# Channel attention of a two-layer decoder on one Trainium2 core: turned scores signalled head by head, and two VectorE instructions moved behind the negation

## The chip, the cores and the metric

The kernel runs on one core of one Trainium2 chip, as one launch. The metric is device time in microseconds (us) of that core, the median over several runs. The engines are TensorE (PE; its weight loads are listed as PEld), VectorE (DVE), ScalarE (ACT), GpSimd (POOL) and SyncE (SP), whose queue issues the DMAs. A "q" behind an engine's name is its sequencer.

## The reference, cut to what matters

The whole reference is a stack of six sublayers on `x` (32, 64, 256), each with a layer norm in front and added back to `x`. The edited part is the fifth, attention over channels:

```python
def _L1_xattn_ref(qkv, y):            # both (32, 64, 256)
    N_HEADS = 16
    bs, width, length = qkv.shape     # 32, 64, 256
    ch = width // N_HEADS             # 4
    q = qkv.reshape(bs * N_HEADS, ch, length)
    k = v = y.reshape(bs * N_HEADS, ch, -1)
    scale = 1.0 / math.sqrt(math.sqrt(ch))
    weight = jnp.einsum('bct,bcs->bts', q * scale, k * scale)
    weight = jax.nn.softmax(weight.astype(jnp.float32), axis=-1)
    a = jnp.einsum('bts,bcs->bct', weight, v)
    return a.reshape(bs, -1, length)

x = x + _L1_xattn_ref(_layernorm(x, axis=-1), ctx_2048)
```

There are 512 heads of 4 channels. Each head has a 256 x 256 matrix of scores, a softmax over it, and a product with the 4 channels of the context.

## The kernel before, in words

**Tiling.** The 2048 tokens are 16 tiles of 128 rows (TILES), 32 heads each. A tile is worked on in 8 slots (CH_SETS), a slot being 4 heads, one in each group of 32 partitions (CH_RGS). Half a tile is 4 slots (CH_HALF). There are 128 slots and 32 halves. Queries and keys are split into f16 parts and laid out by many small DMAs (qp and kp, a ring of 4 tiles).

**Two passes over the scores.** `scores` (L1496) makes the scores of two heads with queries on the partitions (L1502), and VectorE takes each row's maximum (`top`, L1589 to L1593: a reduction of 128 x 1024 values). After 4 slots the 32 columns of maxima are transposed by TensorE (L1547), negated by VectorE into `mT` (L1616), and brought by a DMA (`load_max`, L1431 to L1434) into row 31 of each group of the queries. `scores_turned` (L1506) then makes the same scores with keys on the partitions and the maximum subtracted, since row 31 takes part in the contraction (L1510). ScalarE takes the exponential of each head (L1578), and TensorE multiplies by the values, with a row of ones for the totals (L1558).

**The order of the work.** It is written out by hand in steps n, two to a slot. `tensor_step` (L1514) issues the scores of pair n%2 of slot t = n//2, the turned scores of slot b, 6.5 slots behind (CH_B_LAG = 13 steps), the transpose at the first step of every fourth slot, and a half of the value product of slot c, 8 slots behind (CH_C_LAG = 16). All instructions of an engine run in the order written. Scores use two pairs of PSUM banks in turn, and the transpose takes a turn in that order too (`bank`, `a_first`, `a_turn`, `a_second`). Turned scores use a ring of three banks T, a bank to a head. The waits that matter:

- TensorE, before any score matmul of a step: `s_maxed` (the pair of banks has been read), and `s_exped` for both heads of the pair of turned scores (L1531 to L1533). The four matmuls of scores and the four of turned scores are interleaved (L1534 to L1542), and one count of `s_scoredT` tells of both heads.
- ScalarE: `s_scoredT` for the pair (L1574), then a head's exponential. Once a half it copies the output out of PSUM (L1587).
- VectorE, `vector_step` (L1605): the maximum of the step; at every fourth slot the negation; in the second step of the sixth slot of a tile `invert` (L1595, the reciprocal of the totals of two tiles ago, which waits for their load); in the second step of the fourth slot `measured` (L1601, the layer-norm statistics of three tiles ago, L227 in a helper, which wait for `s_finished`).
- SP, `sync` (L1430), one iteration per tile n: the maxima of the odd half, a weight block of the next stage (`stage`, L186 in a helper), values (`load_v`, L1428, which waits for `s_vset` of GpSimd), the store of an odd half's output (`store_out`, L1438), keys (L1347), the totals of tile n-2 (`load_total`, L1445, which waits until the output has been stored), five query loads (L1423), the maxima of the even half (L1434), a weight block, an output store, four query loads, the store of the reciprocals (`store_inverse`, L1449, which waits for `invert`), three query loads, and the load of output and reciprocals of tile n-2 (`load_out`, L1455 and L1456).
- GpSimd, `gpsimd` (L1687), one iteration per tile: the normalised queries of tile+2, splitting of weight blocks, the values of the even half (`set_v`, L1678), `finish` of tile-2 (L1683 multiplies by the reciprocals, L1685 adds to `x` and counts `s_finished`), then the values of the odd half, for which SP's `load_v` waits.

"Even" and "odd" below mean the half: the even half of a tile is its first, and its negation falls at t % 8 == 4; the negation of the odd half falls at t % 8 == 0 of the next tile.

Of the kernel before, what the change touches and what calls it, by code (L numbers as in the profile page):

```python
# [15 lines left out]
P = 128  # L16
B, S, D = 32, 64, 256
TOKENS = B * S
KD = D // P
TILES = TOKENS // P  # L20
# [1351 lines left out]
def channel_stage(core, keys, moe, jobs=(), first=0):  # L1372
# [39 lines left out]
    def bank(user):  # L1412
        return A[user % 2]
# [3 lines left out]
    def load_q(sp, tile, parts):  # L1417
        sp.wait_ge(s_lo, tile + 1)
        if tile >= CH_RING:
            sp.wait_ge(s_scoredT, 2 * CH_SETS * (tile - CH_RING + 1))  # L1420
        for n in parts:
            p, ch = n // CH_CH, n % CH_CH
            sp.dma_start(qp[n:P:32, tile % CH_RING], xs[ch:P:CH_CH, tile % 2, p % 2]).then_inc(q_in[tile % 2], 16)  # L1423
# [6 lines left out]
    def sync(sp):  # L1430
# [33 lines left out]
        for n in range(TILES + 3):  # L1464
            if 0 <= 2 * n - 1 < CH_HALVES:
                load_max(2 * n - 1)
            stage(2 * n - 1)
            if 2 <= n + 1 < TILES:
                load_v(sp, n + 1)
            if n == 3:  # L1470
                moe.load_constants(sp)
            if 0 <= 2 * n - 3 < CH_HALVES:
                store_out(2 * n - 3)
            if CH_KEYS_AHEAD <= n + 2 < TILES:
                sp.wait_ge(s_scoredT, 2 * CH_SETS * max(0, n + 2 - CH_RING + 1))
                sp.wait_ge(k_in[n % 2], 16 * CH_RGS * (n // 2 + 1))
                keys.load(sp, n + 2, k_in[n % 2])
            if 0 <= n - 2 < TILES:
                load_total(n - 2)
            if n + 2 < TILES:  # L1480
                load_q(sp, n + 2, range(5))
            if 2 * n < CH_HALVES:
                load_max(2 * n)
            stage(2 * n)
            if 0 <= 2 * n - 2 < CH_HALVES:
                store_out(2 * n - 2)
            if n + 2 < TILES:
                load_q(sp, n + 2, range(5, 9))
            if 0 <= n - 2 < TILES:
                store_inverse(n - 2)  # L1490
            if n + 2 < TILES:
                load_q(sp, n + 2, range(9, CH_KEYROWS))
            if 0 <= n - 2 < TILES:
                load_out(n - 2)
# [8 lines left out]
                                    kp[rows, tile % CH_RING, set8, :], start=True, stop=True)  # L1503
        return last

    def scores_turned(t, pair, u):  # L1506
        tile, set8 = t // CH_SETS, t % CH_SETS
        for g in (2 * pair, 2 * pair + 1):
            rows = slice(32 * g, 32 * (g + 1))
            last = nc.tensor.matmul(ps[:, T[(t * CH_RGS + g) % len(T)], u * D:(u + 1) * D], kp[rows, tile % CH_RING, set8, u * P:(u + 1) * P],  # L1510
                                    qp[rows, tile % CH_RING, set8, :], start=True, stop=True)
        return last

    def tensor_step(pe, n):  # L1514
        t, pair = n // 2, n % 2
        tile = t // CH_SETS
        b, b_pair = (n - CH_B_LAG) // 2, (n - CH_B_LAG) % 2
        if t < CH_SLOTS:
            if n % (2 * CH_SETS) == 0:
                pe.wait_ge(q_in[tile % 2], 16 * CH_KEYROWS * (tile // 2 + 1))  # L1520
                pe.wait_ge(k_in[tile % 2], 16 * CH_RGS * (tile // 2 + 1))
            user = (a_first, a_second)[pair](t)
            if user >= 2:
                pe.wait_ge(s_maxed, user - 1)
        if 0 <= b < CH_SLOTS:
            if b == 0 and b_pair == 0:
                pe.wait_ge(*keys.accumulated)
            if b % CH_HALF == 0 and b_pair == 0:
                half = b // CH_HALF
                pe.wait_ge(m_in[half % 2], 16 * (half // 2 + 1))  # L1530
            done = b * CH_RGS + 2 * b_pair + 2 - len(T)  # L1531
            if done > 0:
                pe.wait_ge(s_exped, done)  # L1533
        for u in range(KD):  # L1534
            if t < CH_SLOTS:
                last = scores(t, pair, u)
                if u == KD - 1:
                    last.then_inc(s_scored, 1)
            if 0 <= b < CH_SLOTS:
                last = scores_turned(b, b_pair, u)  # L1540
                if u == KD - 1:
                    last.then_inc(s_scoredT, 1)  # L1542
        if pair == 0 and t % CH_HALF == 0 and 0 < t <= CH_SLOTS:
            half = t // CH_HALF - 1
            user = a_turn(half)
            pe.wait_ge(s_maxed, max(user - 1, a_second(t - 1) + 1))
            nc.tensor.transpose(ps[0:32, bank(user), 0:P], m[:, half % 2].rearrange("p g s u -> p (g s u)"), core.ident).then_inc(s_scored, 1)  # L1547
        c, u = (n - CH_C_LAG) // 2, (n - CH_C_LAG) % 2
        if 0 <= c < CH_SLOTS:
            half, j = c // CH_HALF, c % CH_HALF  # L1550
# [19 lines left out]
    def scalar(act):  # L1570
        for b in range(CH_SLOTS + CH_HALF):
            for g in range(CH_RGS):
                if b < CH_SLOTS:
                    act.wait_ge(s_scoredT, 2 * b + g // 2 + 1)  # L1574
                    if g == 0 and b >= 3:
                        act.wait_ge(s_mixed, b - 2)
                    n = b * CH_RGS + g
# [27 lines left out]
    def vector_step(dve, n):  # L1605
# [4 lines left out]
        if pair == 0 and t % CH_HALF == 0 and t > 0:  # L1610
# [3 lines left out]
            if half >= 2:  # L1614
                dve.wait_ge(m_in[half % 2], 16 * (half // 2))
            nc.vector.tensor_scalar(mT[:, half % 2], ps[0:32, bank(user), 0:P], -1.0, None, ALU.mult).then_inc(s_maxed, 1)  # L1616
        if pair == 1 and t % CH_SETS == 5 and tile >= 2:
            invert(dve, tile - 2)
        if pair == 1 and t % CH_SETS == 3 and tile >= 3:
            measured(dve, tile - 3)  # L1620

    def settle_tiles(dve, tiles):
        done, count = settle(core, dve, f"ch{tiles[0]}", 3, tiles)
# [937 lines left out]
```

## Time and profile before

| what | value |
|---|---|
| median of 3 runs | 1916.67 us (1914.07 to 1920.19) |
| the profiled execution | 1911.81 us |
| its span, first to last instruction | 1910.0 us |
| PE busy | 1707.1 us (89%), 15840 instructions |
| DVE busy | 1489.9 us (78%), 2884 instructions |
| ACT busy | 1031.2 us (54%), 2056 instructions |
| POOL busy | 720.3 us (38%), 965 instructions |
| the edited stage | about 1143 to 1502 us of the span |

The shares are means over six sublayers with different limits, so they don't tell what limits the edited stage. A line is that of the kernel; L227 and L186 are lines of helpers. Times in the rows count from the start of the span.

### The profile page before, as it was taken

The page shows a single profiled execution, that of the slowest core. Times are in us where ns is not written, and L with a number is a line of the kernel's source. Part 1 is how long each engine was busy: PE and PEld are TensorE (multiplying, and loading weights), DVE is VectorE, ACT ScalarE, POOL GpSimd, SP SyncE. Part 2 cuts the span into 40 slices and gives each one's busy share as a digit, 9 for nine tenths or more (in the row PEclk, how much of TensorE's full clock was granted, in tenths as well). Part 3 has the DMA queues.
Part 4 walks back from the last instruction along what each step waited for, and adds up shares of the span by engine and source line. Part 5 has one row for each costly group of instructions (what it writes and reads, how often), then busy time and mean ns, then how long its engine had stood idle before and what let it go on. Part 6 is the DMA issues. An engine that isn't in the chain of part 4 may idle for free.

```text
span 1910.0 us, 43448 instructions
## 1 busy us (share of the span) xinstructions
PE 1707.1 (89%) x15840; PEld 1004.0 (53%) x15840; DVE 1489.9 (78%) x2884; ACT 1031.2 (54%) x2056; POOL 720.3 (38%) x965
## 2 busy tenths in 40 slices
PE   5999999689999999979977996777777889999998
PEld 2656665347777777755544551222222356656555
DVE  6866666579989899857886889999999478676654
ACT  3665655345555555534436765888888533323222
POOL 4635321387677677612345453444531000000000
PEclk9999999889999999989989997999999999999999
DMA  9601110000000000000001211333321023222121
GB/s 254 177 24 51 29 41 2 17 23 12 10 13 14 7 10 4 2 9 1 1 1 36 59 38 52 94 91 96 96 72 41 17 76 96 88 63 72 63 83 50
DMA packets 87662, 94.92 MB, mean 50 GB/s; under 512 B 17568, under 2 KB 63264, under 8 KB 87456
## 3 DMA queue, kind: packets, MB, share of 16 engines
q1 hardware_dynamic: 83712, 87.76, 16.3%
q8 instruction: 128, 2.10, 0.5%
q10 hardware_dynamic: 2976, 2.32, 0.5%
q0 software_dynamic: 768, 2.10, 0.4%
q14 instruction: 78, 0.64, 0.1%
HBM read 78.51 MB, written 10.22 MB: 46 GB/s over the span
## 4 chain that ended last, share of the span: by engine, by line
DVE 23%; PE 22%; issue 6%; POOL 3%; ACT 1%; DVEq 0%; POOLq 0%; ACTq 0%
PE ps L275 18%; DVE arena L1592 14%; POOL arena L1147 2%; PE ps L1859 1%; PE ps L1502 1%; PE ps L1856 1%; DVE arena L2440 1%; DVE arena L2436 0%; DVE arena L1201 0%; DVE arena L244 0%; POOL arena L2013 0%; DVE arena L2371 0%; DVE arena L2369 0%; DVE arena L1952 0%; ACT arena L2312 0%
## 5 line engine op out<-in xcount | busy, mean ns | idle before, releaser
L275 PE MATMUL ps<-arena 128*128 128x512 f16 (+6 forms) x6464 | 1090.9, 324 | 54.6 <-POOL arena L1147 9.6
L275 PEld LDWEIGHTS ps<-arena 128*128 128x128 f16 (+1 forms) x6464 | 602.1, 99 | 442.0 <-issue 37.8
L1578 ACT ACTIVATE arena<-ps 128x512 f32<-128x512 f32 x512 | 278.6, 598 | 71.1 <-PE ps L1510 48.5
L1592 DVE TENSOR_REDUCE arena<-ps 128x4 f32<-128x1024 f32 x256 | 305.3, 1218 | 10.8 <-PE ps L1502 10.5
L1502 PE MATMUL ps<-arena 31*128 31x256 f16 x1024 | 102.2, 275 | 72.7 <-ACT arena L1578 52.1
L1558 PE MATMUL ps<-arena 128*32 128x256 f32 x2048 | 164.1, 392 | 2.7 <-ACT arena L1587 0.6
L2430 DVE TENSOR_TENSOR arena<-ps,arena 128x512 f32<-128x512 f32 x96 | 66.1, 688 | 126.8 <-ACT arena L2322 111.6
L2322 ACT ACTIVATE arena<-ps 128x512 f32<-128x512 f32 x96 | 57.1, 596 | 176.9 <-PE ps L275 176.4
L1502 PEld LDWEIGHTS ps<-arena 31*128 31x128 f16 x1024 | 34.8, 92 | 187.6 <-DVE arena L1592 151.0
L1051 POOL TENSOR_TENSOR arena<-arena 128x512 f32<-128x512 f32 x96 | 98.8, 1043 | 45.1 <-DVE arena L221 44.0
L652 POOL TENSOR_TENSOR arena<-arena 128x256 f32<-128x256 f32 x64 | 39.5, 617 | 180.4 <-DVE arena L617 180.4
L508 ACT ACTIVATE arena<-ps,arena 128x512 f32<-128x512 f32 x64 | 44.0, 687 | 113.6 <-PE ps L275 113.6
L1510 PE MATMUL ps<-arena 32*128 32x256 f16 x1024 | 101.0, 275 | 0.9 <-ACT arena L1578 0.2
L2312 ACT ACTIVATE arena<-arena 128x512 f16<-128x512 f32 x96 | 60.1, 626 | 73.7 <-DVE arena L2436 73.3
L1147 POOL TENSOR_TENSOR arena<-arena 128x512 f16<-128x512 f32 x32 | 50.2, 1575 | 113.3 <-ACT arena L1304 109.9
L197 POOL TENSOR_TENSOR arena<-arena 128x256 f16<-128x256 f32 (+5 forms) x72 | 86.1, 1196 | 5.8
L1065 POOL TENSOR_TENSOR arena<-arena 128x256 f32<-128x256 f32 x80 | 58.2, 728 | 74.4 <-DVE arena L982 74.1
L916 ACT ACTIVATE arena<-ps 128x512 f16<-128x512 f32 x64 | 38.2, 597 | 81.5 <-PE ps L842 81.5
L195 POOL CAST arena<-arena 128x256 f16<-128x256 f32 (+5 forms) x72 | 45.3, 629 | 96.6 <-DMA arena<-in_L_ffn_gate_up_proj 67.3
L981 DVE TENSOR_TENSOR arena<-ps,arena 128x512 f32<-128x512 f32 x80 | 54.9, 686 | 31.7 <-ACT arena L911 24.4
L1056 POOL TENSOR_TENSOR arena<-arena 128x512 f32<-128x512 f32 x64 | 67.5, 1055 | 27.9 <-DVE arena L1017 27.8
L565 DVE TENSOR_TENSOR arena<-ps,arena 128x512 f16<-128x512 f32 x64 | 43.8, 684 | 39.1 <-ACT arena L497 39.1
(203 smaller groups left out, 2931.1 us busy)
## 6 DMA issues: line engine op xcount, KB each, us to landing
arena<-moe_cw SPq DMA_DIRECT2D x64, 192.0 KB, 2.8
arena<-moe_cw SPq DMA_DIRECT2D x64, 128.0 KB, 2.9
arena<-in_L_ffn_gate_up_proj SPq DMA_DIRECT2D x16, 384.0 KB, 3.4
ch_out<-arena SPq DMA_DIRECT2D x32, 128.0 KB
arena<-moe_cw SPq DMA_DIRECT2D x64, 64.0 KB, 2.7
ch_keys<-arena SPq DMA_DIRECT2D x48, 64.0 KB, 2.0
arena<-ch_keys SPq DMA_DIRECT2D x64, 48.0 KB
arena<-arena SPq DMA_DIRECT2D x192, 16.0 KB
```

The lines of the kernel that those rows point to most:

```text
L197: nc.gpsimd.tensor_tensor(lo, raw, hi, ALU.subtract).then_inc(core.s_split, 1)
L275: last = nc.tensor.matmul(out, a, b, start=start and n == 0, stop=stop and n == len(pairs) - 1, skip_group_check=not group)
L1051: nc.gpsimd.tensor_tensor(a4, a4, spread(rms[:, s % 2, u * CROSS_KVH:(u + 1) * CROSS_KVH], CROSS_HD), ALU.mult).then_inc(scaled.sem, 1)
L1056: nc.gpsimd.tensor_tensor(prob[:, k % 2], e[:, k % 2], spread(inv[:, k % 2, :], CROSS_KEYS), ALU.mult).then_inc(probs.sem, 1)
L1147: nc.gpsimd.tensor_tensor(hT[1][:, k % FFN_MEMBERS], h[:, k // FFN_MEMBERS % 2, k % FFN_MEMBERS], hT[0][:, k % FFN_MEMBERS], ALU.subtract) ...
L1502: last = nc.tensor.matmul(ps[:, bank(user) + n, u * D:(u + 1) * D], qp[rows, tile % CH_RING, set8, u * P:(u + 1) * P], kp[rows, tile % CH_ ...
L1510: last = nc.tensor.matmul(ps[:, T[(t * CH_RGS + g) % len(T)], u * D:(u + 1) * D], kp[rows, tile % CH_RING, set8, u * P:(u + 1) * P], qp[ro ...
L1558: last = nc.tensor.matmul(ps[32 * g:32 * (g + 1), O, 0:D], vz[:, half % 2, u, g, j, :], pT[:, c % 3, g, u, :], start=j == 0 and u == 0, st ...
L1578: nc.scalar.activation(pT[:, b % 3, g], ps[:, T[n % len(T)], :].rearrange("p (u t) -> p u t", u=KD), ACT.Exp, scale=CH_SCALE).then_inc(s_e ...
L1592: nc.vector.tensor_reduce(m[:, half % 2, 2 * half_pair:2 * half_pair + 2, j, :], ps[:, bank(user):bank(user) + 2, :].rearrange("p g (u s) ...
L2312: nc.scalar.activation(hT[0][:, b % 4, :], h[b % MOE_HELD], ACT.Copy).then_inc(s_hi, 1)
L2430: nc.vector.tensor_tensor(h[n % MOE_HELD], ps[:, U[n % 2], :], silu[:, n % 2, :], ALU.mult).then_inc(s_gated, 1)
```

## The change

Three things, all in the channel stage:

- TensorE: the turned scores of the pair's first head stay interleaved with the scores, behind a wait for that head's bank alone; those of the second head are issued after the transpose, behind a wait of their own, and ahead of the value product, which is last in the step. Each head counts `s_scoredT`, and every wait on it (ScalarE's, and those of SP before query and key loads) is rescaled from 2 to 4 counts a slot.
- VectorE: `invert` moves from the second step of slot 5 of a tile to directly behind the negation at slot 4.
- VectorE: `measured` moves from the second step of slot 3 to directly behind the negation at slot 0 of the tile, for the same tile-3.

```diff
     def load_q(sp, tile, parts):
...
-            sp.wait_ge(s_scoredT, 2 * CH_SETS * (tile - CH_RING + 1))
+            sp.wait_ge(s_scoredT, CH_RGS * CH_SETS * (tile - CH_RING + 1))
...
             if CH_KEYS_AHEAD <= n + 2 < TILES:
-                sp.wait_ge(s_scoredT, 2 * CH_SETS * max(0, n + 2 - CH_RING + 1))
+                sp.wait_ge(s_scoredT, CH_RGS * CH_SETS * max(0, n + 2 - CH_RING + 1))
...
-    def scores_turned(t, pair, u):
+    def scores_turned(t, g, u):
         tile, set8 = t // CH_SETS, t % CH_SETS
-        for g in (2 * pair, 2 * pair + 1):
-            rows = slice(32 * g, 32 * (g + 1))
-            last = nc.tensor.matmul(ps[:, T[(t * CH_RGS + g) % len(T)], u * D:(u + 1) * D], kp[rows, tile % CH_RING, set8, u * P:(u + 1) * P],
-                                    qp[rows, tile % CH_RING, set8, :], start=True, stop=True)
-        return last
+        rows = slice(32 * g, 32 * (g + 1))
+        return nc.tensor.matmul(ps[:, T[(t * CH_RGS + g) % len(T)], u * D:(u + 1) * D], kp[rows, tile % CH_RING, set8, u * P:(u + 1) * P],
+                                qp[rows, tile % CH_RING, set8, :], start=True, stop=True)
...
         b, b_pair = (n - CH_B_LAG) // 2, (n - CH_B_LAG) % 2
+
+        def bank_free(g):
+            done = b * CH_RGS + g + 1 - len(T)
+            if done > 0:
+                pe.wait_ge(s_exped, done)
+
...
-            done = b * CH_RGS + 2 * b_pair + 2 - len(T)
-            if done > 0:
-                pe.wait_ge(s_exped, done)
+            bank_free(2 * b_pair)
         for u in range(KD):
             if t < CH_SLOTS:
                 last = scores(t, pair, u)
                 if u == KD - 1:
                     last.then_inc(s_scored, 1)
             if 0 <= b < CH_SLOTS:
-                last = scores_turned(b, b_pair, u)
+                last = scores_turned(b, 2 * b_pair, u)
                 if u == KD - 1:
                     last.then_inc(s_scoredT, 1)
...
             nc.tensor.transpose(ps[0:32, bank(user), 0:P], m[:, half % 2].rearrange("p g s u -> p (g s u)"), core.ident).then_inc(s_scored, 1)
+        if 0 <= b < CH_SLOTS:
+            bank_free(2 * b_pair + 1)
+            for u in range(KD):
+                last = scores_turned(b, 2 * b_pair + 1, u)
+            last.then_inc(s_scoredT, 1)
         c, u = (n - CH_C_LAG) // 2, (n - CH_C_LAG) % 2
...
-                    act.wait_ge(s_scoredT, 2 * b + g // 2 + 1)
+                    act.wait_ge(s_scoredT, CH_RGS * b + g + 1)
...
             nc.vector.tensor_scalar(mT[:, half % 2], ps[0:32, bank(user), 0:P], -1.0, None, ALU.mult).then_inc(s_maxed, 1)
-        if pair == 1 and t % CH_SETS == 5 and tile >= 2:
-            invert(dve, tile - 2)
-        if pair == 1 and t % CH_SETS == 3 and tile >= 3:
-            measured(dve, tile - 3)
+            if t % CH_SETS == CH_HALF and tile >= 2:
+                invert(dve, tile - 2)
+            if t % CH_SETS == 0 and 3 <= tile < TILES:
+                measured(dve, tile - 3)
```

## Rows read from the trace of the kernel before

**Rows 1.** Chain of waits, 1130 to 1560 us, shares by line.

```profile
by line: DVE arena L1592 63.3%; issue 10.7%; PE ps L275 10.1%; PE ps L1502 3.2%; DVE arena L1599 1.7%; PE ps L1558 1.1%; POOL arena L2013 1.0%; ACT arena L1578 0.8%; DVE arena L244 0.6%; ACT L2322 0.6%; DVE arena L227 0.5%; PE ps L2207 0.5%
```

**Rows 2.** Table of lines, 1143 to 1502 us: busy us, mean ns, idle before.

```profile
L1592 DVE TENSOR_REDUCE arena<-ps 128x4 f32<-128x1024 f32 x256 | 305.3, 1218 | 10.8 <-PE ps L1502 10.5 <-DVE arena L221 0.2
```

**Rows 3.** Timeline, DVE, 1149 to 1156 us: start, us, instruction, idle before.

```profile
1149.62 5.73 DVE L1592 TENSOR_REDUCE arena<-ps 128x4 f32<-128x1024 f32 x5
```

**Rows 4.** Timeline, DVE, one tile from 1314 us, and the last maximum.

```profile
1314.09 0.27 DVE L1616 TENSOR_SCALAR arena<-ps 32x128 f16<-32x128 f32 x1
1314.66 8.51 DVE L1592 TENSOR_REDUCE arena<-ps 128x4 f32<-128x1024 f32 x7 [0.30 <-PE ps L1502]
1323.08 0.42 DVE L227 BATCH_NORM_STATS2 arena<-arena 128x6 f32<-128x256 f32 x1
1323.41 1.21 DVE L1592 TENSOR_REDUCE arena<-ps 128x4 f32<-128x1024 f32 x1
1324.54 0.27 DVE L1616 TENSOR_SCALAR arena<-ps 32x128 f16<-32x128 f32 x1
...
1328.68 0.54 DVE L1599 RECIPROCAL arena<-arena 128x64 f32<-128x64 f32 x1
...
1334.75 0.27 DVE L1616 TENSOR_SCALAR arena<-ps 32x128 f16<-32x128 f32 x1
...
1478.01 1.22 DVE L1592 TENSOR_REDUCE arena<-ps 128x4 f32<-128x1024 f32 x1
```

**Rows 5.** Timeline, one step from 1357 us, first ACT, then PE.

```profile
1357.24 1.09 ACT L1578 ACTIVATE arena<-ps 128x512 f32<-128x512 f32 x2
...
1358.46 0.60 ACT L1578 ACTIVATE arena<-ps 128x512 f32<-128x512 f32 x1
...
1357.99 0.28 PE L1502 MATMUL ps<-arena 31*128 31x256 f16 x2 [0.25 <-ACT arena L1578]
...
1358.10 0.28 PE L1502 MATMUL ps<-arena 31*128 31x256 f16 x2
1358.12 0.27 PE L1510 MATMUL ps<-arena 32*128 32x256 f16 x2
1358.32 0.42 PE L1558 MATMUL ps<-arena 128*32 128x256 f32 x4
```

**Rows 6.** Timeline, SP's queue, 1313 to 1336 us, DMAs issued.

```profile
1314.01 0.57 SPq L1456 DMA_DIRECT2D arena<-ch_inverse  x1
...
1319.23 0.39 SPq L1428 DMA_DIRECT2D arena<-in_ctxT  x1
...
1323.69 0.62 SPq L1445 DMA_DIRECT2D arena<-ch_out  x1
...
1327.36 0.56 SPq L1434 DMA_DIRECT2D arena<-arena  x1
...
1331.38 0.45 SPq L1449 DMA_DIRECT2D ch_inverse<-arena  x1
...
1334.48 0.57 SPq L1456 DMA_DIRECT2D arena<-ch_inverse  x1
```

**Rows 7.** Timeline, POOL, the final add of four tiles.

```profile
1235.56 0.72 POOL L1685 TENSOR_TENSOR arena<-arena 128x256 f32<-128x256 f32 x1
...
1317.88 0.73 POOL L1685 TENSOR_TENSOR arena<-arena 128x256 f32<-128x256 f32 x1
...
1401.20 0.72 POOL L1685 TENSOR_TENSOR arena<-arena 128x256 f32<-128x256 f32 x1
...
1442.47 0.73 POOL L1685 TENSOR_TENSOR arena<-arena 128x256 f32<-128x256 f32 x1
```

**Rows 8.** Timeline, PE, 1479 to 1480 us, steps without scores.

```profile
1479.59 0.64 PE L1558 MATMUL ps<-arena 128*32 128x256 f32 x8
1480.16 0.39 PE L1510 MATMUL ps<-arena 32*128 32x256 f16 x4
```

**Rows 9.** DMA issues, whole span: KB each, us from issue to landing.

```profile
ch_inverse<-arena SPq DMA_DIRECT2D x16, 32.0 KB, 2.5
```

## The prediction, made before the changed kernel ran

> **What bounds the kernel now.** I read the time and the span first: the profiled execution took 1911.81 us (span 1910.0), 4.86 us below the median of the runs, 1916.67. The sum is made against 1911.81 and then carried to the median. Only the stage of channel attention is edited, about 1143 to 1502 us. The chain of that stretch lies to 63.3% on VectorE's maximum over scores, L1592 [rows 1], and the table of lines has 256 of these at 1218 ns each [rows 2]. So VectorE seems to be the bound. The timeline corrects this. While no turned scores are in flight, five maxima take 5.73 us from the first start to the last end [rows 3]; with 1.22 for the last one that is (5.73 - 1.22) / 4 = 1.13 us apart. In the steady part seven take 8.51 us [rows 4]: 1.215 apart. The 0.085 us comes from a ring between ScalarE and TensorE [rows 5]. An exponential starts at 1357.24 and takes 0.60. It frees the bank for which the whole step on TensorE waits, scores included, and the score matmuls start at 1357.99. The last turned matmul starts at 1358.12 and takes 0.27, one signal then tells of both heads, and the next exponential starts at 1358.46. That is 1.22 us a step.
>
> A second loop hides behind this one. SP's queue and GpSimd fetch each tile's output back, and [rows 6, 7] have to be read together. SP issues the load of the inverse (L1456) at 1314.01. GpSimd's final add (L1685) runs from 1317.88 for 0.73, to 1318.61. Only then does SP get past its wait for the values (L1428, 1319.23). There follow the stores and key loads, the load of the totals (L1445, 1323.69), query loads, the load of the even half's maxima (L1434, 1327.36), the store of the inverse (L1449, 1331.38), and L1456 again at 1334.48. That turn took 20.47 us; over eight turns L1685 goes from 1235.56 to 1401.20, 20.71 each. VectorE's tile, from one odd negation to the next, is 1334.75 - 1314.09 = 20.66 [rows 4]. The two loops are equally long, and the second hardly waits for the first: the even negation ends at 1324.54 + 0.27 = 1324.81, 2.55 us before SP takes it up.
>
> **Part 1, heads signalled one at a time.** The ring is now over three banks, one head each, and the scores no longer stand behind the second bank. Two exponentials take 1.09 us with 0.60 for the second [rows 5], so ScalarE can start one every 0.49, 0.98 a step: not the bound. TensorE's step cost, in the old order, 0.33 from the first score matmul to the first of the value product (1357.99 to 1358.32, [rows 5]) and 0.57 from there to a next step that nothing holds (1479.59 to 1480.16, [rows 8]): 0.90. The second head now adds one or two rounds of 0.11 (1357.99 to 1358.10): 1.01 to 1.12. The added wait could cost a bubble of about 0.09, the 0.20 between 1358.12 and 1358.32 less one round; then it is up to 1.21. I take 1.12, since the rows show no bubble between matmuls of one kind; VectorE then sets 1.13. Behind the added wait stands the value product; it needs exponentials of older slots, so it isn't later than its inputs. The count of signals doubles, for which I see no cost.
>
> In each half turn two more matmuls come between the transpose and the value product. A change from 32-row to 32-column matmuls costs that same 0.09; two more of them in 31 half turns are 5.6 us if nothing hides them. VectorE has the reciprocal or the statistics to do at that place, so I take nothing and keep 5.6 as the far end. The Trainium skill (TensorEngine Tiling (Array Packing), Key Properties) says that switching the tiling mode drains the array, which speaks against this order; the trace agrees, with 0.09 us for one switch, and the sum by that rule would be the far end.
>
> **Part 2, the reciprocal behind the even negation.** After each negation VectorE stands 0.30 us for the second pair's scores [rows 4]. The reciprocal takes 0.54 (1328.68), of which 0.08 lies under its neighbour, as for the statistics, 0.42 long and 0.33 to the next start (1323.08 to 1323.41). So 0.30 of its 0.46 is hidden. But it needs the totals: issued at 1323.69 [rows 6], landed some 2.5 us later, the median to landing of the inverse's store, the nearest transfer of 32 KB [rows 9]. That is 1326.2, and the negation ends at 1324.81: at the old phase it would wait 1.4 us, 20 us over 14 tiles. I take nothing, since part 3 puts VectorE later against SP: totals land 1323.69 + 2.5 - 1318.61 = 7.6 us after L1685 ends, and the negation comes 9.7 us after it. The store of the inverse (1331.38) already stands 2.2 us and more behind the reciprocal in SP's order, so SP gains nothing from an earlier one.
>
> **Part 3, the statistics behind the odd negation.** This decides. They wait for L1685 of three tiles before. Until now they ran at 1323.08, 4.5 us after L1685's end at 1318.61. Behind the negation of 1314.09 they are wanted at 1314.36, 4.25 us before that end. Behind them on VectorE stand the second pair's maximum and all that follows, and so TensorE and ScalarE. VectorE waits, and the two loops become one. From F, the end of L1685:
> - to the statistics 0.05 (a hop; [rows 5] have 0.07 from matmul to exponential, the other end is nothing), the statistics 0.33, eight maxima 7 x 1.13 + 1.14 = 9.05, the even negation 0.27, the hop to SP 0.05: 9.75 to L1434;
> - SP alone reached it 1327.36 - 1318.61 = 8.75 after F;
> - from there to the next F as before: 20.71 - 8.75 = 11.96.
>
> The new turn is 21.71 us, 1.00 longer. VectorE's own tile would be 16 x 1.13 + 0.46 + 0.33 + 2 x 0.19 (0.27 less 0.08) = 19.25. What parts 1 and 2 win goes into the wait.
>
> **The sum.** Ahead of the first wait there is a gain: a half was 1334.75 - 1324.54 = 10.21 and becomes 9.05 + 0.57 (1314.09 to 1314.66) = 9.62. Two to three such halves reach SP before the first L1685: -1.5. Eight turns: +8.0. Two more, to the L1685 of 1442.47 [rows 7], where the weight loads are over: +1.8 (two of 1.00 less a little). That F comes at 1443.20 + 8.3 = 1451.5. The next finish isn't met: it is due 18 to 20 us on, VectorE 19.25. So the last statistics start at 1451.5 + 0.05 + 19.25 = 1470.8, the next maximum at 1471.1, and the last one 14 x 1.13 + 0.46 + 0.19 = 16.5 later, 1487.6. It was at 1478.01 [rows 4]: +9.6. The next stage opens on VectorE's work behind it, so this passes on. The trailing steps may give back 0.5 (nothing to 2). Total +9.1: 1920.9 for the profiled execution, 1925.8 against the median.
>
> **The rivals.**
> (a) The loops stay apart, since L1685 comes in time or SP's part shrinks. Then 19.25 replaces 20.71 in eleven turns, -16.1, and with -1.5 the time is 1899; with half of it 1908. Against it speak the 4.25 us. Chance 0.12.
> (b) One loop, but SP's stretch comes out about 1 us shorter, as its wait for the stored output (before 1323.69) may end sooner at the new phase. Then the turns stay 20.7 and the time is 1916. Chance 0.17.
> (c) Worse than the forecast: a step on TensorE is above 1.13, say 1.21, or the ring lives on. The eight maxima between F and SP's load then cost 0.6 more, 6.6 in eleven turns, and the first and last halves lose a gain of 3: 1935. Chance 0.13.
> (d) The forecast, turns of 21.4 to 22.0: 1920 to 1931. Chance 0.58.
>
> **How the numbers follow.** 0.3%, 5.75 us, is about what a measurement of this kernel can tell from no change. Of (d), 0.48 lies above that and 0.10 within; of (b), 0.13 is within and 0.02 on either side; (c) is slower, (a) faster. Slower 0.63, same 0.23, faster 0.14. The range, 1912 to 1935, takes in (d), most of (b) and half of (c), and leaves (a) out.
>
> **What would show it.** Right: about 2.4 us of idle time before most of the 13 statistics, released by L1685; L1685 every 21.7 us; SP waiting about 1 us for the negation at the even L1434; maxima 1.13 apart. Wrong: no such wait (then (a)), L1685 every 20.7 us (then (b)), maxima 1.2 apart behind the statistics (then (c)), or the reciprocal waiting for its totals.

## The result and the profile after

The changed kernel takes 1927.05 us (median of 6 runs, 1924.86 to 1931.13) where the kernel before takes 1915.57 us in the runs beside it. The ratio is 1.0068, with a 95% interval of 1.0053 to 1.0083: 0.7% slower. The forecast was 1925.8 and slower. It counted from a median of 1916.67 for the kernel before, so it forecast 9.1 us more; measured are 11.5 us more. The profiled execution took 1925.08 us. These are the span, the busy times and the chain of its page, and then the chain of the page of the kernel before:

```profile
span 1923.3 us, 43386 instructions
...
PE 1734.5 (90%) x15779; PEld 1013.2 (53%) x15840; DVE 1476.9 (77%) x2884; ACT 1026.7 (53%) x2056; POOL 719.6 (37%) x965
...
PE 24%; DVE 15%; issue 6%; POOL 3%; DMA 3%; SPq 3%; ACT 2%; DVEq 0%; POOLq 0%; ACTq 0%
```

```profile
DVE 23%; PE 22%; issue 6%; POOL 3%; ACT 1%; DVEq 0%; POOLq 0%; ACTq 0%
```

The chain now has 3% for DMA and 3% for SP's queue. Neither was in the chain before, nor in that of the stage [rows 1]. VectorE is busy for less time than before though the whole takes longer. The waits between 1165 and 1480 us say where it stands still (engine and line, what it waited for, us in total, times, the longest). SP's own waits follow in the second block:

```profile
DVE arena L227 <- POOL arena L1692: 28.5, 12, 4.3
...
PE ps L1502 <- ACT arena L1585: 0.7, 1, 0.7
```

```profile
SPq L1434 <- DVE arena L1623: 59.7, 26, 9.1
...
SPq L1444 <- DMA ch_out<-arena: 20.8, 12, 2.9
```

The first row of the first block is the one the prediction turned on: VectorE's statistics (L227) wait for GpSimd's final add (L1692, L1685 before), 12 times, 28.5 us, 2.4 each. Before, there was no such row. The second row is what the first part of the change has left of its wait. This is its counterpart in the kernel before:

```profile
PE ps L1502 <- ACT arena L1578: 51.2, 206, 0.8
```

And a little more than one tile of VectorE's timeline, to set beside [rows 4]:

```profile
1344.18 0.27 DVE L1623 TENSOR_SCALAR arena<-ps 32x128 f16<-32x128 f32 x1
1346.62 0.43 DVE L227 BATCH_NORM_STATS2 arena<-arena 128x6 f32<-128x256 f32 x1 [2.17 <-POOL arena L1692]
1346.96 4.64 DVE L1599 TENSOR_REDUCE arena<-ps 128x4 f32<-128x1024 f32 x4
1351.94 4.62 DVE L1599 TENSOR_REDUCE arena<-ps 128x4 f32<-128x1024 f32 x4 [0.34 <-PE ps L1502]
1356.48 0.27 DVE L1623 TENSOR_SCALAR arena<-ps 32x128 f16<-32x128 f32 x1
1356.68 0.53 DVE L1606 RECIPROCAL arena<-arena 128x64 f32<-128x64 f32 x1
1357.14 9.06 DVE L1599 TENSOR_REDUCE arena<-ps 128x4 f32<-128x1024 f32 x8
1366.13 0.27 DVE L1623 TENSOR_SCALAR arena<-ps 32x128 f16<-32x128 f32 x1
1368.46 0.43 DVE L227 BATCH_NORM_STATS2 arena<-arena 128x6 f32<-128x256 f32 x1 [2.07 <-POOL arena L1692]
```

The negation ends at 1344.45, and the statistics start at 1346.62, 2.17 us later. Behind them four maxima take 4.64 us. The eight of the next half take 9.06, which is (9.06 - 1.20) / 7 = 1.12 us apart, no longer 1.215. The reciprocal (L1606) starts 0.20 us after the start of the even negation and waits for nothing. GpSimd's final adds in this stretch:

```profile
1345.75 0.73 POOL L1692 TENSOR_TENSOR arena<-arena 128x256 f32<-128x256 f32 x1
...
1367.59 0.73 POOL L1692 TENSOR_TENSOR arena<-arena 128x256 f32<-128x256 f32 x1
```

The add ends at 1346.48, and the statistics start 0.14 us after. From one such end to the next it is 21.84 us here. From SP's queue, as in [rows 6]:

```profile
1356.78 0.56 SPq L1434 DMA_DIRECT2D arena<-arena  x1
```

The load of the even maxima (L1434) starts at 1356.78, just after the negation of 1356.48, and 10.30 us after the end of the add; before, it stood in SP's own order at 8.75. From there the queue's order is that of before, and the next add ends at 1368.32, 11.54 us on. So the two loops have become one.

### The profile page after: what moved, and what is told of

Read it like the earlier page. It is cut to its first block, busy times and chain, and to the rows that moved or that the text cites. A ratio compares the mean times of both kernels' runs of the same rounds, so it can differ in the third digit from the quotient of the medians.

```text
span 1923.3 us, 43386 instructions
## 1 busy us (share of the span) xinstructions
PE 1734.5 (90%) x15779; PEld 1013.2 (53%) x15840; DVE 1476.9 (77%) x2884; ACT 1026.7 (53%) x2056; POOL 719.6 (37%) x965
## 4 chain that ended last, share of the span: by engine, by line
PE 24%; DVE 15%; issue 6%; POOL 3%; DMA 3%; SPq 3%; ACT 2%; DVEq 0%; POOLq 0%; ACTq 0%
PE ps L275 18%; DVE arena L1599 6%; DMA arena<-ch_inverse 2%; SPq L1423 2%; POOL arena L1147 2%; PE ps L1565 1%; DMA ch_inverse<-arena 1%; PE ps L1866 1%; PE ps L1502 1%; PE ps L1863 1%; DVE arena L2447 1%; DVE arena L2443 0%; POOL arena L1692 0%; DVE arena L1201 0%; POOL arena L1690 0%
## 5 line engine op out<-in xcount | busy, mean ns | idle before, releaser
L1585 ACT ACTIVATE arena<-ps 128x512 f32<-128x512 f32 x512 | 273.5, 598 | 87.2 <-PE ps L1509 85.1
L1599 DVE TENSOR_REDUCE arena<-ps 128x4 f32<-128x1024 f32 x256 | 292.9, 1206 | 4.6 <-PE ps L1502 4.1
L1565 PE MATMUL ps<-arena 128*32 128x256 f32 x2048 | 174.3, 415 | 0.5 <-ACT arena L1594 0.4
L2329 ACT ACTIVATE arena<-ps 128x512 f32<-128x512 f32 x96 | 57.1, 596 | 177.1 <-PE ps L275 176.6
L1502 PE MATMUL ps<-arena 31*128 31x256 f16 x1024 | 107.0, 292 | 46.3 <-DVE arena L1599 44.1
L1509 PE MATMUL ps<-arena 32*128 32x256 f16 x1024 | 132.7, 287 | 0.0
L1502 PEld LDWEIGHTS ps<-arena 31*128 31x128 f16 x1024 | 29.6, 94 | 166.4 <-DVE arena L1599 130.0
```

The lines of the kernel that those rows point to most:

```text
L1502: last = nc.tensor.matmul(ps[:, bank(user) + n, u * D:(u + 1) * D], qp[rows, tile % CH_RING, set8, u * P:(u + 1) * P], kp[rows, tile % CH_ ...
L1509: return nc.tensor.matmul(ps[:, T[(t * CH_RGS + g) % len(T)], u * D:(u + 1) * D], kp[rows, tile % CH_RING, set8, u * P:(u + 1) * P], qp[ro ...
L1565: last = nc.tensor.matmul(ps[32 * g:32 * (g + 1), O, 0:D], vz[:, half % 2, u, g, j, :], pT[:, c % 3, g, u, :], start=j == 0 and u == 0, st ...
L1585: nc.scalar.activation(pT[:, b % 3, g], ps[:, T[n % len(T)], :].rearrange("p (u t) -> p u t", u=KD), ACT.Exp, scale=CH_SCALE).then_inc(s_e ...
L1599: nc.vector.tensor_reduce(m[:, half % 2, 2 * half_pair:2 * half_pair + 2, j, :], ps[:, bank(user):bank(user) + 2, :].rearrange("p g (u s) ...
```

## The experiments

Each kernel was timed in interleaved runs with the kernel before. Beside the time I use one length of the trace: the fourteen tiles from the first tile's odd negation to the fifteenth's, 1169.38 to 1459.62 in the kernel before, 20.73 us a tile. What lies around the stage is left out of it. It is an average over unlike tiles, read from one profiled execution of each kernel, so a tenth or two of it mean little.

| kernel | median us | ratio, interval | us a tile |
|---|---|---|---|
| before | 1913 to 1917 | 1 | 20.73 |
| the change | 1927.05 | 1.0068 (1.0053 to 1.0083) | 21.64 |
| statistics back | 1914.82 | 1.0005 (0.9990 to 1.0021) | 20.87 |
| statistics only | 1932.03 | 1.0086 (1.0058 to 1.0114) | 22.03 |
| heads only | 1916.82 | 1.0014 (0.9995 to 1.0033) | 20.85 |
| reciprocal only | 1913.70 | 0.9997 (0.9980 to 1.0014) | 20.82 |
| statistics of four tiles ago | 1918.88 | 1.0006 (0.9990 to 1.0023) | 20.77 |
| SP's order only, on before | 1914.29 | 0.9996 (0.9981 to 1.0011) | 20.68 |
| SP's order, on the change | 1922.59 | 1.0045 (1.0030 to 1.0061) | 21.73 |
| four tiles ago and SP's order | 1910.80 | 0.9969 (0.9952 to 0.9985) | 20.25 |
| the same, constants late | 1906.49 | 0.9958 (0.9942 to 0.9975) | 19.99 |
| the same, reciprocal back | 1903.30 | 0.9956 (0.9939 to 0.9973) | 19.89 |
| constants late, heads in pairs | 1914.11 | 1.0005 (0.9992 to 1.0018) | 20.69 |

**The statistics back at their old place**, on the changed kernel:

```diff
-            if t % CH_SETS == 0 and 3 <= tile < TILES:
-                measured(dve, tile - 3)
...
+        if pair == 1 and t % CH_SETS == 3 and tile >= 3:
+            measured(dve, tile - 3)
```

> The changed kernel with the statistics put back into the second step of the tile's fourth slot; heads signalled singly and the reciprocal behind the even negation stay. Theory (the statistics' wait merged the two loops): the statistics have no idle time before them, GpSimd's final add comes every 20.7 us again, since SP's own loop is left as the bound, maxima stand 1.13 us apart inside a half, and the 11 turns of 21.8 us fall back to 20.7. VectorE is ahead of SP, so either the reciprocal waits for the totals or TensorE for the even half's maxima. Time 1903 to 1912 us. Rival (the new order on TensorE costs the time: switches between 32-row and 32-column matmuls, a fuller step, lower clock): still slower than before, 1920 to 1927 us.

The slowdown is gone, so the statistics' place is its cause and TensorE's new order isn't. But the time is that of before; the gain that I expected, to 1903 to 1912 us, didn't come. GpSimd's final adds are 20.75 us apart, as before. VectorE, faster now, is held at another place. These are its wait at the reciprocal and, from SP's waits, that for the stored output:

```profile
DVE arena L1606 <- DMA arena<-ch_out: 13.1, 9, 4.2
```

```profile
SPq L1444 <- DMA ch_out<-arena: 21.1, 12, 2.8
```

VectorE waits nine times for the totals that SP loads (13.1 us). SP in turn stands 21.1 us for the landing of the output, a part of its own loop. SP's loop is what is left as the bound; that is a reading of these waits here, and the versions with SP's order changed test it below.

**The statistics alone**, on the kernel before:

```diff
+            if t % CH_SETS == 0 and 3 <= tile < TILES:
+                measured(dve, tile - 3)
...
-        if pair == 1 and t % CH_SETS == 3 and tile >= 3:
-            measured(dve, tile - 3)
```

> The kernel before with the statistics alone moved behind the odd negation. Theory: VectorE waits at 12 or 13 statistics, about 1.5 to 2 us each; from the end of GpSimd's final add to SP's load of the even maxima it is 0.05 + 0.33 + 7 x 1.215 + 1.14 + 0.27 + 0.05 = 10.35 us, since the ring of pairs still holds maxima 1.215 apart, so a turn is 10.35 + 11.96 = 22.3 us, 1.6 longer than 20.7; in eleven turns +17.6 us, less what the hidden 0.30 us give: 1928 to 1936 us, slower than the change with all three parts. Rival (the statistics are harmless, TensorE's order is what costs): 1911 to 1918 us.

It is slower than before by 0.86%, as the theory has it, and slower than the full change a tile (22.03 to 21.64). The rival falls. One assumption was wrong: the maxima behind the wait. This is one wait and the eight maxima behind it in that kernel's timeline:

```profile
1395.81 0.43 DVE L227 BATCH_NORM_STATS2 arena<-arena 128x6 f32<-128x256 f32 x1 [1.69 <-POOL arena L1685]
1396.15 9.12 DVE L1592 TENSOR_REDUCE arena<-ps 128x4 f32<-128x1024 f32 x8
1405.19 0.27 DVE L1616 TENSOR_SCALAR arena<-ps 32x128 f16<-32x128 f32 x1
```

Eight take 9.12 us, 1.13 apart, though the ring of pairs is still there: TensorE's steps in this half start at 1401.06, 1402.27 and 1403.48, 1.21 apart. While VectorE waited, TensorE had got ahead by the scores of a step, and eight maxima don't use up that lead. It is so behind nine of the thirteen statistics; behind the other four, where the granted clock falls to 0.50, the eight take 0.5 to 1.1 us more. So a turn was 22.07, not 22.3.

**Heads alone**, on the kernel before (VectorE's program stays as it was; the cut leaves out the counts of `s_scoredT`, rescaled as in the change):

```diff
-            done = b * CH_RGS + 2 * b_pair + 2 - len(T)
-            if done > 0:
-                pe.wait_ge(s_exped, done)
+            bank_free(2 * b_pair)
...
-                last = scores_turned(b, b_pair, u)
+                last = scores_turned(b, 2 * b_pair, u)
...
+        if 0 <= b < CH_SLOTS:
+            bank_free(2 * b_pair + 1)
+            for u in range(KD):
+                last = scores_turned(b, 2 * b_pair + 1, u)
+            last.then_inc(s_scoredT, 1)
```

> The kernel before with the heads' part alone (issue, wait and signal one head at a time); reciprocal and statistics at their old places. Theory: maxima go from 1.215 to 1.13 us apart, TensorE no longer waits for an exponential ahead of scores; VectorE's tile would be 16 x 1.13 + 0.46 + 0.33 + 2 x 0.57 = 20.0 us, but SP's loop keeps 20.6 to 20.7, so only the tiles before and behind the loop's stretch and what the phase allows are won: 1903 to 1912 us. Rival (drains and a fuller TensorE step): 1917 us or more, maxima 1.2 apart or idle time of VectorE before them.

**Reciprocal alone**, on the kernel before:

```diff
-        if pair == 1 and t % CH_SETS == 5 and tile >= 2:
-            invert(dve, tile - 2)
+            if t % CH_SETS == CH_HALF and tile >= 2:
+                invert(dve, tile - 2)
```

> The kernel before with the reciprocal alone moved behind the even negation. Theory: VectorE reaches it ahead of the totals (issued 1323.69, landed about 1326.2, negation done at 1324.81), so it waits in most tiles, first about 1.4 us and then what keeps VectorE in step with SP's loop of 20.7 us; nothing or up to 2 us is won: 1913 to 1918 us. Rival (no wait, 0.30 us hidden in each of 14 tiles): 4.2 us less than before, 1911 to 1912 us. Rival on the other side (the 1.4 us are paid in each of 14 tiles): 1930 us or more.

With single heads the maxima stand 1.13 apart, and yet a tile takes 20.85 us. Final adds are 20.84 apart. Single heads alone win nothing, and they cost nothing that these runs can tell. The gain that I expected around SP's stretch, 1903 to 1912 us, didn't come, and the median, 1916.82, is within 0.2 us of where my rival began, which also named idle time of VectorE. There is such idle time, but not for the rival's reason. Below are VectorE's waits for scores in this kernel (10.0 us in 31 waits in the kernel before), then the longest of them, with SP's load of the even maxima and TensorE's next matmul, and last an ordinary wait behind a negation:

```profile
DVE arena L1599 <- PE ps L1502: 20.0, 43, 2.1
```

```profile
1226.59 0.56 SPq L1434 DMA_DIRECT2D arena<-arena  x1
...
1228.43 0.28 PE L1502 MATMUL ps<-arena 31*128 31x256 f16 x2 [3.42 <-issue]
...
1228.86 1.23 DVE L1599 TENSOR_REDUCE arena<-ps 128x4 f32<-128x1024 f32 x1 [2.12 <-PE ps L1502]
...
1339.14 8.01 DVE L1599 TENSOR_REDUCE arena<-ps 128x4 f32<-128x1024 f32 x7 [0.30 <-PE ps L1502]
```

The wait behind a negation, where the two added matmuls and the switches are, is 0.30 us as in [rows 4]. The added idle time is in a few long waits. In the longest TensorE stands 3.42 us. The trace names no releaser, but in the kernel this step waits for the landing of the even maxima, which SP issued at 1226.59. So it is SP's queue that VectorE meets. Five of the fourteen tiles are free of such waits and take 19.99 us, where my expectation had 20.0.

The reciprocal alone changes nothing either, as expected, but its wait is small, 4.1 us in five waits, not 1.4 in each tile:

```profile
DVE arena L1599 <- DMA arena<-ch_out: 4.1, 5, 1.3
```

**The statistics of four tiles ago**, on the changed kernel, so that they stay behind the odd negation and don't wait:

```diff
-            if t % CH_SETS == 0 and 3 <= tile < TILES:
-                measured(dve, tile - 3)
+            if t % CH_SETS == 0 and 4 <= tile < TILES:
+                measured(dve, tile - 4)
...
         else:
+            if k == 2:
+                measured(dve, TILES - 4)
             measured(dve, TILES - 5 + k)
```

> The changed kernel, but the statistics behind the odd negation are those of four tiles ago, not three; the thirteenth tile's join the ones left for the next stage. Theory: their release came a whole turn earlier (about 16 us before), so they never wait; SP's own loop, 20.7 us a turn, is the bound that is left, as with the statistics at their old place: 1910 to 1917 us, no more than 0.3% off the kernel before. Rival (SP's loop isn't a bound, the putting back of the statistics merely lost their 0.30 us of cover): VectorE's tile of 19.25 us comes out, 1895 to 1903 us.

The median, 1918.88, lies 2 us above my range, but against the runs beside it (1914.43) the ratio is 1.0006: no difference from the kernel before, as the theory has it, and far from the rival's 1903. It isn't the place on VectorE that costs, but the release that it waits for. The wait at the statistics is gone, and what VectorE waits for now is the totals that SP loads:

```profile
DVE arena L1606 <- DMA arena<-ch_out: 17.0, 11, 4.3
```

**SP's order.** Now the other loop. SP stood for the landing of the output before it loaded the totals; three of the five query loads go ahead of it:

```diff
+            if n + 2 < TILES:
+                load_q(sp, n + 2, range(3))
             if 0 <= n - 2 < TILES:
                 load_total(n - 2)
             if n + 2 < TILES:
-                load_q(sp, n + 2, range(5))
+                load_q(sp, n + 2, range(3, 5))
```

On the kernel before:

> The kernel before with one edit in SP's queue: three of the five query loads are issued ahead of the load of the totals, so that SP doesn't stand about 1.6 us for the landing of the output. Theory of two equal loops: SP's turn falls from 20.7 to about 19.2 us, but VectorE's tile stays at 20.66, so nothing or up to 2 us is won: 1911 to 1917 us, and SP now waits for the negation at the even load of maxima in most tiles. Rival (SP's loop alone is the bound): 11 turns of 1.5 us, 1897 to 1901 us.

SP's waits in the kernel before, and in this one:

```profile
SPq L1434 <- DVE arena L1616: 32.8, 9, 9.0
SPq L1444 <- DMA ch_out<-arena: 19.0, 11, 2.9
```

```profile
SPq L1434 <- DVE arena L1618: 65.2, 27, 9.2
...
SPq L1444 <- DMA ch_out<-arena: 5.6, 2, 2.9
```

The landing costs 5.6 us and no longer 19.0, SP waits 27 times for the negation and no longer 9, and the time is the same. Shortening SP's loop alone is worth nothing, as shortening VectorE's alone was.

On the changed kernel:

> The changed kernel with the three query loads ahead of the load of the totals and nothing else. Theory of the merged loop: the edit shortens a stretch of SP's queue that already ends in a wait for the even negation, about 1.1 us of it per turn; that wait gets longer, and the turn of 21.8 us stays: 1923 to 1929 us. Rival (SP's length is what the statistics wait for): 11 turns shorter by 1.5 us, 1908 to 1913 us.

Its wait at the statistics, and SP's own waits:

```profile
DVE arena L227 <- POOL arena L1694: 27.0, 12, 3.0
```

```profile
SPq L1434 <- DVE arena L1625: 77.3, 28, 9.3
...
SPq L1444 <- DMA ch_out<-arena: 2.8, 1, 2.8
```

SP gets rid of its wait for the landing here too (2.8 us, 20.8 in the changed kernel) and waits more for the negation instead (77.3, 59.7 in the changed kernel). VectorE still waits 27.0 us for the final adds, and a tile takes 21.73. The median, 1922.59, lies 0.4 us below my range, and the interval of the ratio, 1.0045, overlaps that of the change. The merged loop goes through VectorE at this place; the part of SP's queue that the edit shortens isn't in it.

On the version with the statistics of four tiles ago:

> Both: the changed kernel with the statistics of four tiles ago and the three query loads ahead of the load of the totals. Theory of two loops: now both are shorter, VectorE 19.25 us a tile, SP about 19.2, with a wait of a few tenths of VectorE's reciprocal for the totals: turns of 19.4 to 19.8 us, about a microsecond less in each of 12, and 1 to 3 us at the ends: 1898 to 1906 us, faster than every other version. Rival (something third holds the tile at 20.6, such as TensorE's step or DMA traffic): 1911 us or more.

VectorE's wait at the reciprocal (L1608 here):

```profile
DVE arena L1608 <- DMA arena<-ch_out: 10.3, 7, 4.3
```

This is faster than the kernel before, by 0.3%, so both loops together were the bound. My range was missed by 5 us. The tile is 20.25, not 19.6, although six of the fourteen take 19.28, VectorE's own length: from the odd negation at 1235.94 to that at 1255.22, for one. VectorE waits 10.3 us at the reciprocal, of that 4.3 at one place, where SP's queue also loads the constants of the next stage. And what follows the last maximum takes 437.65 us against 432.01. The stretch from 1470 to 1490 us, here and in the kernel before (length; busy us and instructions of PE, PEld, DVE, ACT, POOL; granted clock; DMA share, GB/s), has a clock of 0.74 for 1.00:

```profile
1470.00:1490.00 20.00, 17.15 (x147) 5.70 (x147) 8.78 (x34) 12.61 (x26) 2.05 (x6) 0.74 0.08 23
```

```profile
1470.00:1490.00 20.00, 15.33 (x208) 5.26 (x209) 15.17 (x41) 16.24 (x31) 2.07 (x6) 1.00 0.11 32
```

The two stretches don't hold quite the same work, since the stage ends 6 us earlier here. Two other versions tell what such a fall is worth: with the constants late and with the statistics back the same stretch has 0.74 and 0.75, and there what follows the last maximum takes 434.20 and 433.30 us. So the clock makes about 2 of the 5.6 us at most, and what makes the rest in this one execution stays open.

**Constants late.** The three versions built on it:

```diff
-            if n == 3:
+            if n == 12:
                 moe.load_constants(sp)
...
-            if tile == 4:
+            if tile == 13:
                 moe.set_up(pool)
```

> The version with the statistics of four tiles ago and three query loads ahead of the load of the totals, and in addition the constants of the next stage are loaded in SP's thirteenth iteration and set up in GpSimd's fourteenth, no longer in the fourth and fifth. There the reciprocal of the fourth tile waited 4.3 us for its totals and that turn took 23.0 us. Theory: that wait falls to under 1 us and the last maximum comes 4 to 5 us earlier, since VectorE takes that in time: 1904 to 1908 us. Rival (SP catches up anyway, or the late constants hold the next stage back): no change, 1909 to 1913 us.

The reciprocal's waits fall from 10.3 to 6.5 us. The longest was to fall below 1 us and is 3.3, at the constants' new place, so it has moved more than it has gone:

```profile
DVE arena L1608 <- DMA arena<-ch_out: 6.5, 7, 3.3
```

It comes out at 1906.49; against the version without this edit (1910.80) the intervals overlap, so that this edit is worth 4 us is likely and not shown.

The same with the reciprocal at its old place:

```diff
-            if t % CH_SETS == CH_HALF and tile >= 2:
-                invert(dve, tile - 2)
...
+        if pair == 1 and t % CH_SETS == 5 and tile >= 2:
+            invert(dve, tile - 2)
```

> The same with late constants, but the reciprocal at its old place, in the second step of slot 5. Theory: it never waits for its totals, and costs 0.46 uncovered, of which 0.30 was hidden behind the negation; where it waited up to 2 us per tile in its new place the time is won back. VectorE's tile is 19.6 us and even: within 2 us of the version with the reciprocal behind the negation, 1904 to 1910 us. Rival (the reciprocal's waits lie on the path that bounds the tiles): 3 us or more faster than that version.

The ratio is 0.9956, with 0.9958 for the version before. The median, 1903.30, is 3.2 us lower and 0.7 us below my range, but the intervals nearly coincide: a difference between the reciprocal's two places isn't shown, and one of 3 us isn't ruled out. These two are the fastest versions of the study, 0.4% ahead of the kernel before.

And the constants-late version with the turned scores in pairs, as in the kernel before:

```diff
-            bank_free(2 * b_pair)
+            done = b * CH_RGS + 2 * b_pair + 2 - len(T)
+            if done > 0:
+                pe.wait_ge(s_exped, done)
...
-        if 0 <= b < CH_SLOTS:
-            bank_free(2 * b_pair + 1)
-            for u in range(KD):
-                last = scores_turned(b, 2 * b_pair + 1, u)
-            last.then_inc(s_scoredT, 1)
```

> The same with late constants, reciprocal behind the negation, statistics of four tiles ago and SP's reorder, but TensorE's heads in pairs as in the kernel before. Theory: with SP's loop out of the way the ring of pairs is the bound, maxima 1.215 apart; VectorE's tile is 16 x 1.215 + 0.46 + 0.33 + 0.4 less what catches up, 20.2 to 20.6 us, so 0.8 us a tile slower than with single heads: 1910 to 1915 us. Rival (single heads never paid, SP's reorder alone makes the gain): the same time as with single heads.

With pairs the ring of [rows 5] is back. These are the score matmuls (L1504 here) waiting for an exponential:

```profile
PE ps L1504 <- ACT arena L1580: 51.1, 203, 0.8
```

There are 203 such waits, 51.1 us, and a tile of 20.69 against 19.99. The intervals of the two ratios, 1.0005 and 0.9958, are apart. So single heads are worth 0.7 us a tile, 0.5% of the time, as soon as SP's loop is out of the way, and nothing measurable while it isn't.

## Why the prediction was right

**The loops.** That the two loops were equally long and that the second hardly waits for the first was right. The kernels that shorten only one of them (heads alone, reciprocal alone, SP's order alone, statistics of four tiles ago) and the putting back of the statistics have ratios within 0.15% of 1, with intervals that reach 0.33%. That the second loop is SP's is shown by its order: with VectorE's loop already short, changing it takes the tile from 20.77 to 20.25 us.

**Part 1.** Maxima at 1.13 came as predicted. A step on TensorE at full clock in the changed kernel, and the start of a later one and of the one behind it:

```profile
1352.41 0.28 PE L1502 MATMUL ps<-arena 31*128 31x256 f16 x2
1352.42 0.28 PE L1509 MATMUL ps<-arena 32*128 32x256 f16 x1
...
1352.54 0.48 PE L1509 MATMUL ps<-arena 32*128 32x256 f16 x3
1352.95 0.42 PE L1565 MATMUL ps<-arena 128*32 128x256 f32 x4
...
1356.62 0.28 PE L1502 MATMUL ps<-arena 31*128 31x256 f16 x2
...
1357.53 0.28 PE L1502 MATMUL ps<-arena 31*128 31x256 f16 x2
```

Here the second head adds two rounds: 0.54 from the first score matmul to the value product (1352.41 to 1352.95), where it was 0.33. With the 0.57 behind it the step is 1.11; I took 1.12. That is the long case. The step from 1356.62 to 1357.53 is 0.91, and the second head adds nothing to it. So TensorE had more room than I gave it.

The switches at the transpose stayed covered. The time can't show it, since the interval of the heads alone reaches 1.0033, which is 6.3 us. VectorE's waits can: behind a negation they are 0.30 us with the heads alone, as before, and in the changed kernel all its waits for scores in the stretch are 3.6 us, where they were 10.0. So the far end of 5.6 us wasn't reached. The Trainium skill (TensorEngine Tiling (Array Packing), Key Properties) says that a change of tiling mode drains the array. The rows agree as far as the 0.09 us of the prediction go; here none of it reached VectorE.

**Part 2.** Right in the changed kernel, where the reciprocal never waited. The 20 us that I named for the old phase were far off: alone it waited 4.1 us in all. The longest wait, 1.3 us, is about the 1.4 that I had, but I let it be paid 14 times. VectorE, once held back, is later in the next tile too; that this is why most tiles don't wait is argued and not tested.

**Part 3.** 12 of 13 statistics waited (predicted: most), 2.4 us each (predicted 2.4). The turn, over eight from the second final add to the tenth, is 21.84 us (predicted 21.71, 20.70 before). Its parts: to SP's even load 10.06 on average (predicted 9.75), from there on 11.78 (predicted 11.96). Two errors of opposite sign cancel in part, so that the turn is nearer than its parts.

**The sum.** The last maximum came 12.6 us later (1478.01 to 1490.58), where I had 9.6. The differences are terms of the sum. The early gain of 1.5 us didn't come: the first final add ends at 1213.02 in both. The turn with the constants took 23.91 for 23.26, +0.6. The eight turns cost 9.1 instead of 8.0, the two behind them 1.4 instead of 1.8. The trailing 0.5 wasn't given back; what follows the last maximum took 432.7 for 432.0. In all it is +13.3 between the two profiled executions and +11.5 in the medians, against +9.1. That the forecast of 1925.8 lies only 1.3 us from 1927.05 is in part luck: the median it was counted from, 1916.67, came out 1.1 us lower in more runs.

**The rivals.** (a), that the loops stay apart, is what happens when the statistics don't wait; but its price was wrong. I let VectorE's own 19.25 us a tile come out, 1899 us. The runs without the wait stay at 20.8, since SP's own loop is there whatever VectorE does. The prediction had that loop in its first part and forgot it where the final add merely comes in time; only with a shorter SP part as well do tiles of 19.28 appear, and then in six of fourteen. (c) was wrong in its mechanism as far as the ring goes: in the kernel with the statistics alone, which still has the ring, the maxima behind a wait stand 1.13 apart.

## What to carry to other kernels

An instruction moved into an idle gap brings its wait along: ask when its releaser comes, not only whether the gap is wide enough, because on an engine that runs in order everything behind it pays. Where two loops over different engines take the same time, as here, the second hardly shows in the first one's waits and shortening one is worth nothing; look for the loop in which each step is released by the one before, DMA landings and queue order included, and shorten both. The same edit (single heads) was worth 0% in one surrounding and 0.5% in another.

## What the runs showed of the hardware

I hadn't expected the clock to take part. In the kernel before it is granted in full from 1200 to 1450 us. In the changed one it falls there ten times to half, 1.2 GHz. Eight of the falls stand behind one of VectorE's twelve waits, during which TensorE stands idle; two, near 1232 and 1256 us, don't. Three stretches of the changed kernel (columns as above), and TensorE's timeline in the second:

```profile
1345.00:1348.00 3.00, 1.39 (x24) 0.38 (x16) 1.38 (x2) 1.84 (x4) 2.92 (x7) 1.00 0.48 139
1348.40:1351.60 3.20, 3.20 (x40) 0.69 (x32) 3.20 (x3) 2.17 (x4) 3.03 (x4) 0.50 0.47 129
1352.00:1355.00 3.00, 2.89 (x46) 0.85 (x38) 3.00 (x3) 3.00 (x7) 0.24 (x2) 1.00 0.11 26
```

```profile
1348.23 0.32 PE L1502 MATMUL ps<-arena 31*128 31x256 f16 x2 [1.84 <-DVE arena L1599]
...
1349.73 0.40 PE L1502 MATMUL ps<-arena 31*128 31x256 f16 x2
...
1351.30 0.39 PE L1502 MATMUL ps<-arena 31*128 31x256 f16 x2
```

TensorE was idle for 1.84 us before 1348.23, and 0.50 is the granted clock in the stretch that follows, 1.00 again behind it. A step takes 1.57 us there (1349.73 to 1351.30) and not 1.11, and the fifth maximum behind the wait starts 0.34 us late for that (1351.94 above). The way from the final add to SP's load is 9.83 us in the three of these eight turns where it is shortest, and up to 10.30 in the others, of which this is one; the average is 10.06. The three are those behind which the clock doesn't fall, so 0.23 of the 0.31 us by which this part came out longer than predicted goes with the falls. From 1200 to 1450 us the clock is 0.93 in the mean, in the kernel before 1.00. The changed kernel's row, then that of before:

```profile
1200.00:1450.00 250.00, 207.53 (x2953) 63.83 (x2953) 221.20 (x229) 199.32 (x388) 105.24 (x188) 0.93 0.31 85
```

```profile
1200.00:1450.00 250.00, 195.30 (x3116) 61.00 (x3115) 241.95 (x243) 213.11 (x410) 108.15 (x198) 1.00 0.31 87
```

The falls belong to TensorE's idle time and not to the change as such: with the statistics alone, on pairs, the same stretch has 0.97, with the heads alone 0.96, where the wait of 3.42 us shown above is followed by a clock of 0.50, and the kernels with only the reciprocal moved or only SP's order changed have 1.00. What a fall costs where VectorE doesn't wait for TensorE behind it was not measured apart.

The start of the stage, 1143 to 1180 us, ran at half clock for longer as well, in the execution shown: 0.58 in the mean, and 0.72 in the kernel before. How much of that lies with the change, which is hardly at work before 1160, and how much with the single execution is open; the other kernels had 0.58 to 0.68 with single heads and 0.68 without, and no run was made to separate the two.
